# One load each for hx, hy and the correction rows, and the first segment's stores on two queues

## What is computed

```
xn  = x*bn1_g/sqrt(1+eps) + bn1_b
q   = grouped 1x1 conv of xn                       # 8 groups of 16 channels
off = gelu(depthwise conv 6x6, stride 4, of q)     # 8x8 positions per group
off = tanh(off_pw_w . off) * 4                     # an x and a y shift for each position
kv  = bilinear sample of xn at grid + off          # 64 keys per group
k, v = grouped 1x1 convs of kv
pos  = grid_q - grid_kv                            # for every query (1024) and key (64), x and y
bias = sign(pos) * log1p(|pos|)
bias = relu(bias @ cpb_w1 + cpb_b1)                # 2 -> 32
bias = relu(bias @ cpb_w2 + cpb_b2)                # 32 -> 32
bias = bias @ cpb_w3 + cpb_b3                      # 32 -> 1
attn = softmax(q.k/4 + bias);  out = attn . v
x = x + out_w.out + out_b;  x = x + mlp_w2.gelu(mlp_w1.bn2(x) + mlp_b1) + mlp_b2
```

## Time and profile before

| what | us |
|---|---|
| median of three runs | 909.36 |
| the profiled execution | 908.36 |
| its span, first to last instruction | 906.3 |
| TensorE busy in the span | 814.3 |
| VectorE busy | 711.1 |
| ScalarE busy | 675.8 |
| GpSimd busy | 69.1 |

### The profile page before, as it was taken

How to read it: one execution, slowest core, us unless ns; L and a number is a source line. 1 busy time by engine, 2 the same in 40 slices (tenths; PEclk the granted TensorE clock), 3 DMA queues, 4 the chain that set the end, 5 groups by cost and what they waited for, 6 DMA issues and landing times.

```text
span 906.3 us, 27727 instructions
## 1 busy us (share of the span) xinstructions
PE 814.3 (90%) x12452; PEld 229.1 (25%) x12452; DVE 711.1 (78%) x493; ACT 675.8 (75%) x773; POOL 69.1 (8%) x40
## 2 busy tenths in 40 slices
PE   3299998899999999789999999888999999999986
PEld 2122222222222222223222222222222222222222
DVE  4799798798877588888885879889887758989821
ACT  2368787978786688896876878897877768888862
POOL 2110021210000004030000001220000000000000
PEclk8589998999999999999999999999999999999999
DMA  4401010020120102002020100102011010200001
GB/s 150 95 15 48 5 31 21 8 53 4 25 44 12 50 3 50 8 3 55 2 64 14 48 4 26 27 7 54 4 34 40 8 50 2 71 5 2 2 15 36
DMA packets 23781, 27.06 MB, mean 30 GB/s; under 512 B 15600, under 2 KB 17520, under 8 KB 23664
## 3 DMA queue, kind: packets, MB, share of 16 engines
q1 hardware_dynamic: 23664, 25.29, 10.4%
HBM read 23.05 MB, written 2.10 MB: 28 GB/s over the span
## 4 chain that ended last, share of the span: by engine, by line
issue 58%; PE 26%; POOL 6%; ACT 5%; DVE 3%; DMA 0%; ACTq 0%; SPq 0%; POOLq 0%
PE pair L824 9%; PE scores L842 8%; POOL conv_prod L325 4%; POOL big L432 3%; ACT h L452 3%; PE pair L798 2%; DVE h L600 2%; PE pair L975 2%; PE scores L853 1%; PE pair L950 1%; PE pair L932 1%; PE pair L966 1%; ACT big L554 1%; PE scores L938 1%; ACT L554 0%
## 5 line engine op out<-in xcount | busy, mean ns | idle before, releaser
L600 DVE TENSOR_TENSOR h<-hx,hy 128x2048 f32<-128x2048 f32 x256 | 582.3, 2302 | 77.5 <-PE pair L824 73.3
L452 ACT ACTIVATE h<-pair 128x1024 f32<-128x1024 f32 x512 | 517.3, 1023 | 148.0 <-PE pair L798 104.8
L824 PE MATMUL pair<-h,wts 32*32 32x512 f32 x8192 | 301.2, 605 | 21.3 <-DVE h L600 6.7
L842 PE MATMUL scores<-h,wts 128*32 128x512 f32 x2048 | 275.7, 607 | 0.1
L798 PE MATMUL pair<-fy,u_rows 32*128 32x512 bf16 x1024 | 102.8, 388 | 16.6 <-DMA fy<-fy_dram 16.6
L824 PEld LDWEIGHTS pair<-h,wts 32*32 32x32 f32 x8192 | 66.3, 103 | 83.3 <-ACT h L452 35.3
L798 PEld LDWEIGHTS pair<-fy,u_rows 32*128 32x128 bf16 x1024 | 26.3, 91 | 234.2 <-issue 234.2
L842 PEld LDWEIGHTS scores<-h,wts 128*32 128x32 f32 x2048 | 42.1, 108 | 157.0 <-issue 148.5
L325 POOL TENSOR_TENSOR conv_prod<-qpad,wts 128x288 f32<-128x288 f32 x16 | 34.0, 2150 | 416.3 <-ACT qpad L479 416.3
L432 POOL TENSOR_TENSOR big<-big,hat_x 128x512 f32<-128x512 f32 x16 | 32.4, 2054 | 127.7 <-DVE big L698 127.7
L462 ACT ACTIVATE probs<-scores,wts 128x512 f32<-128x512 f32 x32 | 22.0, 688 | 23.8 <-PE scores L842 23.5
(11 more groups left out here) (89 smaller groups left out, 358.5 us busy)
## 6 DMA issues: line engine op xcount, KB each, us to landing
hx<-features_dram SPq DMA_DIRECT2D x64, 128.0 KB, 2.8
hy<-features_dram SPq DMA_DIRECT2D x64, 128.0 KB, 3.2
att_den<-reciprocals_dram SPq DMA_DIRECT2D x8, 256.0 KB
wts<-weights_dram SPq DMA_DIRECT2D x2, 960.0 KB, 7.7
x<-x_dram SPq DMA_DIRECT2D x2, 512.0 KB, 5.5
fy<-fy_dram SPq DMA_DIRECT2D x64, 6.0 KB
fy<-fy_dram SPq DMA_DIRECT2D x64, 4.0 KB
fy<-fy_dram SPq DMA_DIRECT2D x64, 2.0 KB
```

The source lines that it names most:

```text
L452: emptied("z", 2 * g + j, act.activation(h2[j][g % H2_BUFS][:].rearrange("p r n -> p (r n)"), pair_of("z", 2 * g + j)[:], ACT.Relu))
L600: dve.tensor_tensor(h1[g % H1_BUFS][:].rearrange("p c (y x) -> p c y x", x=W), hx[unit % 2][:, :, t].unsqueeze(2).broadcast_to([128, CT, H ...
L824: ins = pe.matmul(z_of(g, r)[32 * c:32 * (c + 1)], w(l, "w2")[key_rows(r), key_rows(r)], h1[g % H1_BUFS][key_rows(r), c], start=r >= 2, st ...
L842: ins = pe.matmul(scores[phase % 2][32 * r:32 * (r + 1)], w(l, "w3")[:, 32 * t:32 * (t + 1)], h2[rows[0] // 2][step % H2_BUFS][:, r % 2], ...
```

## The change

`hx` and `hy` of a unit are now loaded by one DMA each. Its source pattern has three dimensions, 4 rows, then 32 repeats, then 1024 numbers, and its destination is all 128 partitions. The correction rows `fy` are kept in DRAM in the layout in which TensorE reads them, 128 rows of 2 KB for a segment, and one load brings them for all 4 units. For that the stores are six instead of three, one for each of the six products of parts, with 4 x 32 pieces of 256 bytes each. The rows of ones are written to DRAM once, early. In the first segment the three stores of part 0 are issued by ScalarE and the other three by SyncE, ahead of the feature loads. All 8 convolution products of the first segment are on VectorE.

```diff
 PROLOGUE = {
-    "act": ["q_out", "image_t_out", "conv_gelu", "offset_tanh", "features", "spread_out"] + ["distances"] * 4,
-    "dve": ["norm1", "w1y_rows", "conv_products", "conv_products", "conv_sum", "conv_sum", "positions", "features_sign",
+    "act": ["q_out", "image_t_out", "conv_gelu", "offset_tanh", "features", "store_fy_first",
+            "spread_out"] + ["distances"] * 4,
+    "dve": ["norm1", "w1y_rows", "conv_products_all", "conv_sum", "conv_sum", "positions", "features_sign",
             "fy_weights", "hidden_terms"],
-    "pool": ["conv_products", "conv_products", "hat_products", "hat_products"],
+    "pool": ["hat_products", "hat_products"],
 }
...
-        fy = [sb(f"fy{p}", [128, STRIDES, H], BF16) for p in range(2)]
+        fy = [sb(f"fy{p}", [128, STRIDES, PAIRS, H], BF16) for p in range(2)]
...
+        def fy_rows(seg, k):
+
+            d = fy_dram[seg]
+            n = STRIDES * PAIRS * H
+            return bass.AP(tensor=d.tensor, offset=d.offset + CT * n * k, ap=[[32 * n, ROWS], [PAIRS * H, 32], [1, PAIRS * H]])
...
-                sp.wait_ge(fy_ready, 3 * (seg + 1))
-                for s in range(3):
-                    sp.dma_start(fy_dram[seg, s].rearrange("u k q -> k u q"), fy_part[s][:]).then_inc(fy_stored, 16)
+                for k, (part, _) in enumerate(PRODUCTS):
+                    if seg or part:
+                        sp.wait_ge(fy_ready, 3 * seg + part + 1)
+                        sp.dma_start(fy_rows(seg, k), fy_part[part][:]).then_inc(fy_stored, 16)
...
                     f = features_dram[seg, xy, pair]
-                    for r in range(ROWS):
-                        src = bass.AP(tensor=f.tensor, offset=f.offset + CT * STRIDES * r * W,
-                                      ap=[[0, HID], [1, CT * STRIDES * W]])
-                        sp.dma_start(dst[HID * r:HID * (r + 1)].rearrange("p c t q -> p (c t q)"), src)\
-                            .then_inc(feat_loaded[p], 16)
...
+                    n = CT * STRIDES * W
+                    src = bass.AP(tensor=f.tensor, offset=f.offset, ap=[[n, ROWS], [0, HID], [1, n]])
+                    sp.dma_start(dst[:].rearrange("p c t q -> p (c t q)"), src).then_inc(feat_loaded[p], 16)
+
+            def load_fy(seg):
+
+                sp.wait_ge(fy_stored, 16 * len(PRODUCTS) * (seg + 1))
+                sp.wait_ge(ones_stored, 16)
+                if seg >= 2:
+                    wait_filled(sp, "z", 2 * SEG_STEPS * (seg - 1) - 1)
+                sp.dma_start(fy[seg % 2][:].rearrange("p t u q -> p (t u q)"), fy_dram[seg]).then_inc(fy_loaded, 16)
...
+            def store_fy_first(seg):
+                act.wait_ge(fy_ready, 1)
+                for k, (part, _) in enumerate(PRODUCTS):
+                    if part == 0:
+                        act.dma_start(fy_rows(seg, k), fy_part[0][:]).then_inc(fy_stored, 16)
...
+            def conv_products_all(seg):
+                wait_emptied(dve, "q", seg)
+                for oy in range(HD):
+                    conv_product(dve, seg, oy).then_inc(conv_multiplied[oy // (HD // 2)], 1)
```

More of the change, by code:

```diff
@@ L254, in build @@
         ones_set = sem("ones_set")
+        ones_stored = sem("ones_stored")
         xn_ready = sem("xn_ready")
@@ L269, in build @@
         feat_loaded = [sem(f"feat_loaded{p}") for p in range(2)]
-        fy_loaded = [sem(f"fy_loaded{p}") for p in range(2)]
+        fy_loaded = sem("fy_loaded")
         terms_ready = sem("terms_ready")
@@ L398, in _ @@
             sp.dma_start(wts[1][:, EARLY:], weights[1][:, EARLY:]).then_inc(late_loaded[1], 16)
+            sp.wait_ge(ones_set, 1)
+            n = STRIDES * PAIRS * H
+            rows = bass.AP(tensor=fy_dram.tensor, offset=fy_dram.offset + FY_ROWS * n,
+                           ap=[[32 * n, SEGS * ROWS], [1, (32 - FY_ROWS) * n]])
+            sp.dma_start(rows, fy[0][:].rearrange("p t u q -> p (t u q)")).then_inc(ones_stored, 16)
             for unit in range(UNITS):
@@ L402, in _ @@
                     store_features(seg)
-                    load_features(unit)
                     store_fy(seg)
-                else:
-                    load_features(unit)
-                load_fy(unit)
+                load_features(unit)
+                if pair == 0:
+                    load_fy(seg)
                 if pair < 2 and seg:
@@ L436, in _ @@
                 pool.memset(qpad[p][:], 0.0).then_inc(borders_zeroed, 1)
-            for p in range(2):
-                pool.memset(fy[p][:], 1.0).then_inc(ones_set, 1)
+            pool.memset(fy[0][:], 1.0).then_inc(ones_set, 1)
             pool.wait_ge(early_loaded[0], 16)
@@ L558, in _ @@
                       "offset_tanh": offset_tanh, "features": features, "spread_out": spread_out,
+                      "store_fy_first": store_fy_first,
                       "distances": distances, "attend_out": attend_out,
@@ L654, in features_sign @@
                 if seg:
-                    dve.wait_ge(fy_stored, 16 * 3 * seg)
+                    dve.wait_ge(fy_stored, 16 * len(PRODUCTS) * seg)
                 y = feat[:, PAIRS:2 * PAIRS]
@@ L718, in hidden_terms @@
                 l, p = unit // PAIRS // B, unit % 2
-                dve.wait_ge(feat_loaded[p], 16 * 2 * ROWS * (unit // 2 + 1))
+                dve.wait_ge(feat_loaded[p], 16 * 2 * (unit // 2 + 1))
                 dve.tensor_scalar(hx[p][:], hx[p][:], w(l, "w1x"), w(l, "b1"), ALU.mult, ALU.add).then_inc(terms_ready, 1)
@@ L796, in correction @@
                 unit, h, t = g // UNIT_STEPS, g // STRIDES % 2, g % STRIDES
-                y = fy[unit % 2][key_rows(r), t, H // 2 * h:H // 2 * (h + 1)]
+                y = fy[unit // PAIRS % 2][key_rows(r), t, unit % PAIRS, H // 2 * h:H // 2 * (h + 1)]
                 return pe.matmul(z_of(g, r), u_rows[unit // PAIRS // B][key_rows(r)],
@@ L809, in corrections @@
                     if g % UNIT_STEPS == 0:
-                        pe.wait_ge(fy_loaded[unit % 2], 16 * 3 * ROWS * (unit // 2 + 1))
+                        pe.wait_ge(fy_loaded, 16 * (unit // PAIRS + 1))
                         pe.wait_ge(u_ready, unit // PAIRS // B + 1)
@@ L1087 @@
     features = nc.dram_tensor("features_dram", (SEGS, 2, PAIRS, 2 * NKV, W), F32, kind="Internal").ap()
-    fy_parts = nc.dram_tensor("fy_dram", (SEGS, 3, PAIRS, 2 * NKV, H), BF16, kind="Internal").ap()
+    fy_rows = nc.dram_tensor("fy_dram", (SEGS, 128, STRIDES * PAIRS * H), BF16, kind="Internal").ap()
     reciprocals = nc.dram_tensor("reciprocals_dram", (2 * SEGS, G, HALF), F32, kind="Internal").ap()
-    build(nc, *args, out, features, fy_parts, reciprocals)
+    build(nc, *args, out, features, fy_rows, reciprocals)
     r = run_bass_kernel_spmd(nc, [arrays], core_ids=[0])
```

2 lines of the change are left out of this document (1 added, 1 removed).

## The result

The change makes the kernel slower. The medians are 921.81 us after and 910.53 before (four runs each); the ratio is 1.0132, with an interval of 1.0097 to 1.0166. Run once more beside other kernels, the changed kernel gave 918.75 against 909.47: 1.0106 (1.0085 to 1.0127). The forecast was +5.7 us, and 921.0 at the upper end of the range; the median lies just above it. The direction was right and the size half of what came.

What follows compares the result with a forecast made beforehand. VectorE's prologue chain, hanging on the landing of `hx` and `hy`, was taken to set step 3. Landing at 26.7 + 11.2 + 0.3 + 0.4 = 38.6 against 32.91 gave +5.7 us: 915.1 us on the median, range 910 to 921.

Steps and rivals of the forecast that it cites:

- The place: Prologue, first 55 us: VectorE's chain from the landing of `hx` and `hy` sets step 3 and all that follows.
- the four engines and their rate: `hx` and `hy` loads: 4 of 16 DMA engines at 23.4 GB/s each, 11.2 us for 1.049 MB.
- a longer wait of TensorE at step 3: Prologue: TensorE starts near 42.6, as before, then waits for VectorE some 6 us instead of 0.62.
- the sum itself: VectorE's chain: `hx` and `hy` land at 38.6 against 32.91, +5.7 us, giving 915.1 on the median.
- rival C: TensorE before step 3: the pause lowers its clock, two steps at half clock, 3.4 us more, 918.5; chance 0.12.
- Cost nothing: SyncE's three store issues ahead of the loads: hidden by the feature store's landing; without that cover 1.5 us.
- the stores' work on the four engines: Six bf16 stores on the loads' DMA engines: 0.3 us left when `hx` begins, ends 0 and 2.5.
- The convolution: First segment, all eight products on VectorE: sums begin at 14.9, -0.8 us for all stages behind.
- A: `hx` and `hy` loads use all 16 engines, land at 31.4, chain 1.5 earlier, 907.9; chance 0.12.
- B: `hx` and `hy` loads: four engines at only 15.2 GB/s each, landing at 44.7, +11.8, 921.2; chance 0.12.
- D: Slack behind step 3 or a saving on SyncE absorbs the delay, 909 to 911; chance 0.06.
- E: Prologue: TensorE's start decides, only `fy` counts, TensorE starts 6 us or so earlier, 903; chance 0.03.

Runs made afterwards that it cites:

- four loads: Changed kernel with `hx` and `hy` again loaded by four DMAs of 32 partitions each; 913.06 against 908.29 us, ratio 1.0041.
- one load alone: Kernel before the change with only `hx` and `hy` loaded by one DMA each; 915.55 against 908.29 us, ratio 1.0073.
- hats ahead: Changed kernel with VectorE's two hats put ahead of the hidden terms of unit 0; 911.28 against 909.47 us, ratio 1.0023.
- together: Changed kernel with four loads each for `hx` and `hy`, hats before hidden terms, correction rows ordered by product, row, key; 907.14 against 909.47 us.
- hats ahead of before: Kernel before the change with only the hats put ahead of the hidden terms; 909.53 against 908.89 us, ratio 1.0005.
- sixteen ways: Changed kernel with the `hx` and `hy` sources as 16 overlapping rows repeated 8 times, so other numbers are loaded; 913.06 against 908.29 us.
- stores spread: Changed kernel with four loads each for `hx` and `hy` and correction rows ordered by product, row, key; 910.96 against 908.89 us.

## Why the prediction was wrong in size

**What held.** The place (the prologue, VectorE's chain from the landing to step 3); the four engines and their rate (101 GB/s measured, 94 expected); a longer wait of TensorE at step 3; a loop that is otherwise untouched. The hidden terms of the profiled execution were to come 5.7 us later. They came 8.58 later, of which 1.3 is the late constants. `fy` was there at 42.19, 0.7 behind the features (forecast 0.5). TensorE's first layer-2 product needs the features too and came 4.2 behind the hidden terms (forecast 4.0), at 45.68 and not at 42.6.

**The step that failed** is the sum itself, which ended with VectorE's chain. The fall of the clock stood beside it as rival C, with a chance of 0.12 and a price of 3.4. It follows from the forecast's own last line (TensorE waits some 6 us), and the rows had shown the clock at 0.50 in the idle time of the prologue; so it belonged into the sum. It cost 2.9 us in one profile (27.32 less 24.40) and 2.1 in the other, and the experiment with useless products took it away. Before the experiments I also gave the fall to the late features. The kernel with four loads shows that an early `fy` suffices.

The price of 3.4 came near by luck. C counts two steps in layer 2 and the last layer; what ran slow behind the pause was layer 2 of step 3 (0.9 more) and the sample (1.7 more), with a little of the last layer. C also says that steps 0 to 2 ran at half clock before the change. Only steps 0 and 1 did: step 2 took 1.17. After the change the first profile has all three at half clock, so steps 0 to 2 took 12.4 us instead of 9.9. With the later start this is why the wait at step 3 was 3.62 us and not some 6.

**Two terms were too small.** "Cost nothing" was said of the three stores ahead of the loads: between the issues of the feature store and of `hx` lie 2.87 us instead of 2.30, 0.6 more. And of the stores' work on the four engines I left 0.3 us. From the issue of `hx` to the hidden terms it took 14.18 in place of the 12.8 of the sum, 1.4 more. The kernel with one load alone, without the stores ahead, took 13.46, so the stores cost 0.7 and not 0.3. The other 1.0 is there without them (13.46 against 12.5), although the rate was the better one of 101 GB/s; what it is stays open. The convolution gave 1.14, where I had 0.8.

**The account.** Features on the way +8.4 (+7.9 in the second profile), convolution -1.14, clock +2.9 (+2.1): +10.2 and +8.9, against medians of +11.3 and +9.3. The rest is within what the runs spread. Two things that come and go, whatever the kernel, belong to that spread: the late constants (1.3 us), and the low clock at the very end. The latter made the last wait 11.8 or 11.9 us instead of 8.9 in four of the 13 profiles (changed, hats ahead, together, hats ahead of before). How often it came in the executions without a profile is not known. For several other kernels (sixteen ways, four loads, together, stores spread, hats ahead of before) the medians lie 1 to 3 us above the same account, the most for sixteen ways, whose profiled execution was the fastest of its runs; this is left open.

**The rivals.** A (all engines) is refuted by the share of 0.25. B (slow because rows repeat) too: an engine moved 25 GB/s. C came, on top of the forecast. D and E did not; E is refuted the hard way, by the kernel in which holding `fy` back helped.

## What to carry to other kernels

Before joining loads into one, look at the outermost dimension of both patterns: a source of 4 rows repeated 32 times runs on 4 of the 16 DMA engines, and the DMA share of a stretch shows it at once. Where two chains meet (here VectorE's and TensorE's at step 3), making one earlier buys nothing but a pause, and a pause of TensorE can cost its clock on top. Shorten both together, or move work out of the longer one into a wait that is there anyway. Putting the hats into VectorE's wait took 0.83% off the changed kernel, at least as much as going back to four loads (0.65%; the intervals overlap); in the kernel before, where VectorE's chain was not alone, it gave nothing.

## What was not expected of the hardware

Three small stores took 8.49 us to issue behind two loads on four engines, instead of 1.53. The slow loads alone are not enough for that: in the changed kernel the three loads issued right behind the same two took 0.34, 0.51 and 0.53 us. What in the stores makes the difference no run here shows. One of four engines moved 25 GB/s (101 / 4), while 16 engines moved 15 each (243 / 16), so the four engines lost less than their number says. Sharing one row is hardly the reason: with sixteen ways each engine has its own of 16 overlapping rows and moved 15 too (236 / 16). What holds all 16 near 240 GB/s stays open. And four hat products of VectorE cost 5.71 us beside GpSimd's and 2.49 without: more than half of VectorE's time there was the company.
